# The last addition of a tile, made by an accumulating transfer instead of by VectorE

## The reference

```
x = x + gnn(layernorm(x), edges)        # three layers, each:
    agg = segment_sum(x[src], dst) / max(degree, 1)
    out = agg @ Wl + bl + x @ Wr ;  x = where(out >= 0, out, a * out)
x = x + moe(layernorm(x))
    cw  = the 2 largest of softmax(x @ Wr + br), 0 for the 6 other experts
    out = sum over 8 experts of  cw[e] * (relu(x @ W1[e] + b1[e]) @ W2[e] + b2[e])
```

## Time and profile before

| | before |
|---|---|
| time, median of 3 runs | 2570.76 us (2570.03 to 2573.92) |
| time of the profiled execution | 2568.55 us |
| its span, first to last instruction | 2566.9 us |
| PE, DVE, ACT, POOL busy | 98%, 74%, 58%, 41% of the span |
| chain that ended last | PE 93%, DVE 3%, DMA 2% |
| mean granted TensorE clock | 0.999 |

### The profile page before, as it was taken

One profiled execution on the slowest core, in us unless ns is written; L12 is line 12 of the kernel. 1 busy time (PEld: TensorE's weight loads), 2 busy tenths in 40 slices (PEclk: granted clock), 3 DMA queues, 4 the chain that ended last, 5 costly groups with the idle time before them and its releaser, 6 DMA issues.

```text
span 2566.9 us, 40265 instructions
## 1 busy us (share of the span) xinstructions
PE 2510.6 (98%) x9906; PEld 1632.6 (64%) x9906; DVE 1900.5 (74%) x5059; ACT 1484.9 (58%) x3471; POOL 1044.4 (41%) x1293
## 2 busy tenths in 40 slices
PE   7999999999999999999999999999999999999999
PEld 3444445555488875555568885554547888888887
DVE  5555555555599976555589995557748999999997
ACT  2322245556288875565458885555525666666665
POOL 2222245555244435555333333555533333333332
PEclk9999999999999999999999999999999999999999
DMA  4444368888355548888735556998843334533331
GB/s 131 132 134 135 132 186 264 273 266 269 103 165 165 164 155 270 268 269 269 235 101 164 161 168 220 326 322 258 273 148 91 99 99 140 165 102 94 102 102 64
DMA packets 208171, 460.91 MB, mean 180 GB/s; under 512 B 34895, under 2 KB 35207, under 8 KB 208004
## 3 DMA queue, kind: packets, MB, share of 16 engines
q0 software_dynamic: 64928, 207.55, 28.1%
q1 hardware_dynamic: 73812, 125.17, 14.1%
q10 hardware_dynamic: 69264, 126.12, 13.4%
HBM read 245.32 MB, written 213.93 MB: 179 GB/s over the span
## 4 chain that ended last, share of the span: by engine, by line
PE 93%; DVE 3%; DMA 2%; ACT 1%; issue 1%; SPq 0%; ACTq 0%; POOL 0%; DVEq 0%; POOLq 0%
PE psY L678 11%; PE psY L796 9%; PE psM L796 9%; PE psH L796 8%; PE psY L692 6%; PE psY L700 6%; PE psY L709 6%; PE psT L658 5%; PE psS L808 4%; PE psS L809 4%; PE psY L883 3%; PE psH L917 3%; PE psH L930 3%; PE psH L921 3%; PE psY L895 3%; PE psY L886 3%
## 5 line engine op out<-in xcount | busy, mean ns | idle before, releaser
L564 POOL DMA_INDIRECT rows<-y_rows,lists x471 | 491.1, 1043 | 468.4 <-PE psS L809 348.0
L1332 DVE TENSOR_TENSOR lows<-rows,highs 128x512 fp32r<-128x512 f32 x471 | 326.0, 692 | 357.6 <-ACT highs L964 348.7
L964 ACT ACTIVATE outs<-psS 128x512 f32<-128x512 f32 x471 | 279.4, 593 | 275.2 <-PE psS L809 265.7
L964 ACT ACTIVATE highs<-rows 128x512 fp32r<-128x512 f32 x471 | 294.7, 626 | 150.7 <-ACT outs L964 105.4
L808 PE MATMUL psS<-highs,sel 128*128 128x512 f32 x471 | 347.0, 737 | 13.8 <-ACT outs L964 8.5
L571 POOL DMA_INDIRECT rows<-sum_rows,nodeI x158 | 211.1, 1336 | 313.0 <-DVE rows L1340 298.2
L678 PE MATMUL psY<-wy,res 128*128 128x512 f32 x632 | 285.9, 596 | 0.7 <-ACT res L964 0.7
L964 ACT ACTIVATE outs<-psY 128x512 f32<-128x512 f32 x237 | 141.7, 599 | 223.3 <-PE psY L678 213.7
L796 PE MATMUL psM<-wz,res 128*128 128x512 f32 x544 | 255.4, 592 | 0.0
L796 PE MATMUL psY<-wz,res 128*128 128x512 f32 x536 | 251.6, 592 | 0.0
L796 PE MATMUL psH<-wz,res 128*128 128x512 f32 x528 | 247.9, 592 | 0.0
(11 more groups left out here) (204 smaller groups left out, 4911.6 us busy)
## 6 DMA issues: line engine op xcount, KB each, us to landing
sum_rows<-outs ACTq DMA_DIRECT2D x471, 256.0 KB, 3.9
y_rows<-outs SPq DMA_DIRECT2D x237, 256.0 KB, 2.0
rows<-in_x POOLq DMA_DIRECT2D x78, 256.0 KB, 3.0
outs<-in_x SPq DMA_DIRECT2D x78, 256.0 KB, 2.6
out_rows<-res SPq DMA_DIRECT2D x78, 256.0 KB, 2.0
rows<-y_rows,lists POOLq DMA_INDIRECT x471, 4.4
z_rows<-res SPq DMA_DIRECT2D x13, 512.0 KB, 5.4
res<-z_rows SPq DMA_DIRECT2D x13, 512.0 KB, 3.9
```

What stands on the lines that cost most here:

```text
L564: pool.indirect_dma_start(out=rows[:, t % RING, :], out_offset=None, in_=y_d, in_offset=bass.IndirectOffsetOnAxis(ap=col(srcT, t), axis=0) ...
L964: act.activation(o, i_, ACT.Copy).then_inc(signal, 1)
L1332: dve.tensor_tensor(lows[:, t % RING, :], rows[:, t % RING, :], highs[:, g, :].bitcast(F32), ALU.subtract)\
```

## The change

`finish` goes from DVE. ACT gets `take_out(k)`, which copies the second product from `psH` into a new SBUF buffer `added`; there is one such buffer. SP stores the tile's own rows to the output (`store_base`) as soon as they are made, some iterations before. POOL gets `add_out(k)`, which adds `added` onto the stored rows in memory by an accumulating transfer. `o_sb` is now signalled by ACT's copy, `o_st` by the accumulating transfer, and `take_out(k)` waits for `o_st` of tile k - 1 because there is one buffer.

```
--- before.py
+++ after.py
@@ -144,6 +144,7 @@
         h_high = nc.alloc_sbuf_tensor_at("h_high", [P, D], F32R, offset=wz_at)
         h_low = nc.alloc_sbuf_tensor_at("h_low", [P, D], F32R, offset=wz_at + 4 * D)
         h_cross = nc.alloc_sbuf_tensor_at("h_cross", [P, D], F32R, offset=wz_at + 8 * D)
+        added = nc.alloc_sbuf_tensor_at("added", [P, D], F32, offset=wz_at + 12 * D)
         xhs = nc.alloc_sbuf_tensor_at("xhs", [P, 2, D], F32R, offset=wy_at)
         xls = nc.alloc_sbuf_tensor_at("xls", [P, 2, D], F32R, offset=wy_at + 8 * D)
         xcs = nc.alloc_sbuf_tensor_at("xcs", [P, 2, D], F32R, offset=hw_at)
@@ -287,6 +288,7 @@
         gchain = sem("gchain")
         cw_made = sem("cw_made")
         pad_set = sem("pad_set")
+        base_st = sems("base_st", 2)
 
         block = ctx.enter_context(nc.Block())
 
@@ -485,11 +487,12 @@
                     each_pair(sp, lambda i, c: store_y(i, c, l + 1), True)
 
 
-            def store_out(k):
+            def store_base(k):
                 t, s, n = node_of(k), k % 2, k // 2
                 r = NR if t == NT - 1 else P
-                sp.wait_ge(o_sb[s], n + 1)
-                sp.dma_start(out[rows_of(t, r)], kept(place(k), r)).then_inc(o_st[s], 16)
+                sp.wait_ge(var_in[s], uses(s) + n + 1)
+                sp.wait_ge(base_st[s], 16 * n)
+                sp.dma_start(out[rows_of(t, r)], kept(place(k), r)).then_inc(base_st[s], 16)
 
             def bring_back(j):
 
@@ -499,15 +502,13 @@
                 sp.dma_start(res[:, AWAY + a:AWAY + a + 2, :], z_d[a * P:(a + 2) * P].rearrange("(t p) d -> p t d", p=P))\
                   .then_inc(z_back, 16)
 
-            for k in range(4, NT):
-                load_own(k)
-                if k >= 6:
-                    store_out(k - 6)
+            for k in range(NT):
+                if k + 4 < NT:
+                    load_own(k + 4)
+                store_base(k)
                 j = k - AWAY - 4
                 if 0 <= j < AWAY // 2:
                     bring_back(j)
-            for k in range(NT - 6, NT):
-                store_out(k)
             all_turns(sp, o_st, 1, 16)
             sp.wait_ge(zero_st, 16)
 
@@ -643,12 +644,24 @@
             gather_own(2, var_in, 1)
             scale_shift(1)
             gather_own(3, var_in, 1)
+            def add_out(k):
+
+                t, s, n = node_of(k), k % 2, k // 2
+                r = NR if t == NT - 1 else P
+                pool.wait_ge(o_sb[s], n + 1)
+                pool.wait_ge(base_st[s], 16 * (n + 1))
+                pool.dma_start(out[rows_of(t, r)], added[0:r, :], accum_op=ALU.add).then_inc(o_st[s], 16)
+
             for k in range(NT):
                 gates(k)
                 if k + 2 < NT:
                     scale_shift(k + 2)
                 if k + 4 < NT:
                     gather_own(k + 4, var_in, 1)
+                if k >= 3:
+                    add_out(k - 3)
+            for k in range(NT - 3, NT):
+                add_out(k)
 
 
         @block.tensor
@@ -1108,11 +1121,19 @@
                 act.wait_ge(down_ps, k + 1)
                 act.activation(psH[:, :], psH[:, :], ACT.Copy, scale=1.0 + 1.0 / STEP).then_inc(down_wide, 1)
 
+            def take_out(k):
+                s, n = k % 2, k // 2
+                act.wait_ge(o_ps[s], n + 1)
+                act.wait_ge(o_st[1 - s], 16 * ((k + 1) // 2))
+                copy(added[:, :], psH[:, :], o_sb[s])
+
             act.wait_ge(mend_add, 2 * LAYERS)
             act.wait_ge(pad_set, 2)
             norm(0)
             x_top(0)
             for k in range(NT):
+                if k >= 3:
+                    take_out(k - 3)
                 if k >= 2:
                     h_top(k - 2)
                 if k + 1 < NT:
@@ -1125,11 +1146,14 @@
                     x_top(k + 1)
                 if k >= 2:
                     widen_down(k - 2)
+            take_out(NT - 3)
             h_top(NT - 2)
             gated(NT - 1)
             widen_down(NT - 2)
             h_top(NT - 1)
+            take_out(NT - 2)
             widen_down(NT - 1)
+            take_out(NT - 1)
 
 
         @block.vector
@@ -1530,11 +1554,6 @@
                 if ahead:
                     after(k_var)
                     variance(s)
-            def finish(k):
-                s, n = k % 2, k // 2
-                dve.wait_ge(o_ps[s], n + 1)
-                dve.tensor_tensor(kept(place(k)), psH[:, :], kept(place(k)), ALU.add).then_inc(o_sb[s], 1)
-
             def step(ins):
 
                 done[0] += 1
@@ -1606,8 +1625,6 @@
 
             x_parts(0)
             for k in range(NT):
-                if k >= 3:
-                    finish(k - 3)
                 if k >= 2:
                     h_parts(k - 2)
                 if k >= 1:
@@ -1615,12 +1632,9 @@
                 experts(k, ahead=(k + 2 < NT))
                 if k + 1 < NT:
                     x_parts(k + 1)
-            finish(NT - 3)
             h_parts(NT - 2)
             gate_parts(NT - 1)
-            finish(NT - 2)
             h_parts(NT - 1)
-            finish(NT - 1)
 
 
 # ---- launch: one core; inputs and outputs as the reference has them ----
```

More of the change, by code:

```diff
@@ L1532, in experts @@
                     variance(s)
[L1533 to L1536, removed]
             def step(ins):
```

## The result

The changed kernel takes 3125.55 us (median of 4 runs, 3123.83 to 3127.35), the kernel before 2572.34 us in the same comparison (2570.03 to 2576.22): a ratio of 1.2157, 95% interval 1.2142 to 1.2172. The forecast was 3174 us, between 3030 and 3360. The span of the profiled execution grew from 2566.9 to 3124.4 us, by 557.5.

What follows compares the result with a forecast made beforehand. PE bounds the kernel before; after the change a closed loop through ACT, DVE, POOL and the transfer takes 16.0 us a tile. Over the stage that adds 602.4 us, the end 3.4, to 2568.55: 3174 us, range 3030 to 3360.

Steps and rivals of the forecast that it cites:

- The bound now: Experts' stage before the change: PE sets the pace at 7.90 us a tile; DVE's dropped pass gives at most 1.5 us.
- The loop: Closed chain from one `take_out` through DVE, POOL and the transfer to the next: 16.0 us a tile.
- copy to DVE's start: ACT: `h_top` starts 0.50 after the copy, `h_high` takes 0.60, DVE starts 0.1 later; 1.20 us.
- DVE's start to the end of the row for `top_set`: DVE from L1455 to the end of L1525, with no extra wait for ACT: 5.71 us.
- from there to the end of POOL's gather: POOL's start 0.12 us after DVE's row, then 3.62 us of its steps through the gather.
- gap ahead of the issue: POOL, between the gather and the accumulating transfer's issue: a gap like the gather's, 0.43 us.
- issue: POOL's issue of the accumulating transfer, taken nearer a plain transfer than a scatter: 0.8 us, bounds 0.58 and 1.28.
- landing from the end of the issue, to ACT's start: Accumulating transfer lands like POOL's scatter, 4.0 us (bounds 2.5 and 5.4), plus 0.1 until ACT starts.
- The lighter iterations and the end: Last four intervals lack some POOL or DVE work and are shorter; then two copies wait for landings, end 16.7 us.
- the rival: PE's clock falls to half when PE idles in the stage, and PE becomes the bound; chance 0.08.
- the floor of 15.8 us: PE's iteration at half clock throughout, 2 x 7.9 us; binds only if the transfer is quicker, giving 3158 us.
- What was put at nothing: SP's earlier store of own rows and `bring_back` waiting for accumulating transfers: claimed never to be the last wait, no cost.

Runs made afterwards that it cites:

- the last kernel: The kernel with the three edits, but for the last three tiles DVE adds and SP stores as before the change: 2567.51 us, ratio 0.9993.
- the kernel with the three edits: Changed kernel with two buffers `added`, POOL's transfer at the head of its iteration, and `h_top` ahead of ACT's copy: 2571.79 us.
- The loops of 13.55 and 13.99 us: Two variants of the changed kernel: POOL's transfer issued ahead of the gather, 3001.46 us; a plain store instead of the addition, 3021.62 us.

## Why the prediction was right

**The bound now.** PE at 7.90 us a tile, DVE nearly as full and worth 1.5 us at most. Confirmed: without DVE's pass and without the new waits the routers stand 7.88 apart, where they stood 7.90, and the last kernel is 2.0 us below before, with an interval that holds 1.

**The loop.** It is there as it was written out, in the order copy, `h_high`, DVE, POOL, transfer, and both ways of opening it bring the time back to within 16 us of before. Its length was forecast at 15.98 and is 15.35 on average. Term by term, from the iteration shown, 2399.36 to 2414.64:

| term | forecast | measured |
|---|---|---|
| copy to DVE's start | 1.20 | 1.12 |
| DVE's start to the end of the row for `top_set` | 5.71 | 5.69 |
| from there to the end of POOL's gather | 3.74 | 3.82 |
| gap ahead of the issue | 0.43 | 0 |
| issue | 0.8 | 1.0 |
| landing from the end of the issue, to ACT's start | 4.1 | 3.65 |
| sum | 15.98 | 15.28 |

Two terms were mis-sized. The gap ahead of the issue, 0.43, is not there: the queued issue follows the gather directly. The landing was counted from the wrong end. I read it from the earlier trace rows as counted from the end of the issue; the copy's start 4.66 us after the start of an issue whose median landing is 4.5 shows that it counts from the start. Issue and landing together, put at 4.8, so take 4.5: the 4.0 of a scatter was 0.5 too short, and the wrong end made it 0.8 too long. That these two errors partly cancelled, to 0.3, is luck. What held back the gather in the earlier trace rows is on record too, in the kernel before:

```profile
L613 POOLq MOVE  x79: 29/29/29, 1909.8 to 2523.0; - x79
```

POOL's sequencer begins with that gather at 1909.8, 4.7 us after the start of the last scatter, which is the maximum of the earlier trace rows; its row starts 0.8 later. I had taken these 0.8 us of POOL's for landing.

The fit of the Trainium skill, DMA: Bandwidth & Descriptors, anatomy of the gpsimd path, 2.6 us for 256 KB, is too short even for the plain store, which landed in 3.2 from the start of its issue; it has no price for the addition. The 72 whole intervals took 1104.9 us and not 1152, and the last four 4.0 less than the 51.1 forecast; the end took 2.2 us more than thought and the first copy came 0.6 later. That leaves 48 us, the difference between 3174 and 3126.

**The lighter iterations and the end.** The last four intervals were put at 14.4, 14.4, 11.5 and 10.8. They took 13.4, 13.4, 10.2 and 10.2, from 3058.43 to 3105.51: 1.0, 1.0, 1.3 and 0.6 less, mostly by the same two terms. The end was put at 5.6, 5.6 and 5.5 and took 7.1, 5.0 and 6.8. The last two copies do not wait for a landing, as I thought, but for PE (L947), and ahead of the first of them PE works at half clock; the same four products took 1.20 us ahead of the last copy:

```profile
3106.74 1.94 PE L930 MATMUL psH<-down_high,h_high 128*128 128x512 f32 x4 [3.95 <-ACT h_high L1115]
```

And behind the last landing stand the 2 us of POOL's last step.

**The clock.** It fell as the rival had it and cost nothing in the loop, as was said: no term of the table is PE's. Once the loop ends it costs something: 7.1 us to the copy of k = 77, where the kernel with the three edits needs 5.5. But the floor of 15.8 us is wrong: it supposed half clock throughout, and the clock comes back while PE works, within the iteration. The loops of 13.55 and 13.99 us show it. The rival rested on the Trainium skill, TensorE: Matmul & The Clock Gate, Part 1, which says both, that idling brings the half rate and that work releases it; I used only the first half.

**What was put at nothing.** SP's early stores, `base_st` and `bring_back`: in none of the kernels do they end a wait of ACT or DVE. The place of `h_top` behind a copy that waits for PE was in the listing, and was not priced; it is worth 13 us once the loop is open (2585.12 against 2572.30). While the loop is closed the same swap is worth some 125 us (428 above before instead of 553), since the copy then waits for the transfer.

## What to carry to other kernels

A wait for a buffer is priced by the whole chain from the moment the buffer is filled to the moment it is free, through every instruction queued ahead of the one that frees it, and not by the transfer. Here a transfer of 4.6 us stood behind 10.6 us of other work that in turn stood behind the copy. Follow such a chain once round; if it comes back to the waiting instruction within one iteration, its length is the time of an iteration. Then there are two cures, a second buffer or an earlier place in the issuing engine's list, and either was enough here; and work taken from an engine that isn't the bound gives nothing, even with every wait mended.

## What the runs showed of the hardware

An addition within a transfer of 128 rows of 2 KB from SBUF to memory, issued by POOL, occupies POOL for 1.00 us against 0.60 for a plain one, and lands 4.5 us after the start of its issue against 3.2. The same transfer issued ahead of the gather landed in 4.1 at the median. Queued directly behind a gather it is issued without a gap, while the gather behind small steps has 0.43 to 0.44 us before it. When POOL issues the kernel's last transfer, plain or adding, the kernel ends 2.2 us after its landing; with SP's store it was 0.5. In a loop in which PE idles for 5.4 us at the median before it works, its granted clock goes between 0.50 and 1.00 within each iteration, 0.84 over the stage, and the loop is none the longer.
